# A convolution and attention network on one core: the steps of all engines in another order

## The reference

```python
# block 1 (after a group norm of 32 channels a group), n = 1024 pixels
xn  = layernorm(x[:, :48])                       # over 48 channels, per pixel
q, k, v = split(bn(w_qkv @ xn))                  # 16, 16, 48 channels
attn = softmax(q.T @ k / 4)                      # 1024 x 1024 per image
y   = bn(w_proj @ relu(concat(v @ attn.T, x[:, 48:])))
# block 2 (after a second group norm)
q, k, v = qkv_w @ x                              # 8 heads of 24 channels, attention over channels
at  = softmax(l2norm(q) @ l2norm(k).T * temperature) @ v
conv_x  = depthwise3x3(conv1x1(v))
t       = conv1x1(at)                            # 32 channels
channel_map = conv1x1(t * conv1x1(mean(t)) * conv1x1(dw7x7_dilated3(dw3x3(t))))
x1, x2  = split(depthwise3x3(conv1x1(conv_x)))   # spatial branch, gelu(x1) * x2
out = proj(at gated by the spatial map + conv_x gated by the channel map)
```

## Time and profile before

| | before |
|---|---|
| time, median of 3 runs | 395.75 us (395.29 to 396.08) |
| the profiled execution: span from first to last instruction | 393.8 us |
| its own time beside the span | not recorded; median less span is 1.95 us |
| TensorE busy | 353.9 us, 90% |
| VectorE busy | 269.3 us, 68% |
| ScalarE busy | 168.3 us, 43% |
| GpSimd busy | 24.1 us, 6% |
| DMA | 12.37 MB, mean 31 GB/s |
| chain that ended last | TensorE 75%, ScalarE 7%, VectorE 6%, SP's queue 4%, DMA 4% |

### The profile page before, as it was taken

One profiled execution on the slowest core, in us unless ns is written; L12 is line 12 of the kernel. 1 busy time (PEld: TensorE's weight loads), 2 busy tenths in 40 slices (PEclk: granted clock), 3 DMA queues, 4 the chain that ended last, 5 costly groups with the idle time before them and its releaser, 6 DMA issues.

```text
span 393.8 us, 5228 instructions
## 1 busy us (share of the span) xinstructions
PE 353.9 (90%) x2098; PEld 180.1 (46%) x2098; DVE 269.3 (68%) x490; ACT 168.3 (43%) x283; POOL 24.1 (6%) x29
## 2 busy tenths in 40 slices
PE   2978989999987998899999989998999889797995
PEld 1736644433465454544445465443244365352431
DVE  5757667551597647796878577889357889748553
ACT  2233054656503248346520775235522574625410
POOL 2030100000003200000000020000100001000000
PEclk9977689999997599999899999997999899969999
DMA  8450000000000001200002102000002111013005
GB/s 254 140 147 2 0 0 2 0 1 2 0 1 2 0 2 28 62 2 2 0 2 75 28 9 52 12 2 0 0 2 80 29 33 33 0 29 64 2 0 160
DMA packets 6069, 12.37 MB, mean 31 GB/s; under 512 B 2078, under 2 KB 2718, under 8 KB 5918
## 3 DMA queue, kind: packets, MB, share of 16 engines
q1 hardware_dynamic: 5532, 11.97, 11.2%
q10 hardware_dynamic: 514, 0.08, 0.1%
HBM read 5.32 MB, written 3.15 MB: 22 GB/s over the span
## 4 chain that ended last, share of the span: by engine, by line
PE 75%; ACT 7%; DVE 6%; SPq 4%; DMA 4%; POOL 2%; issue 1%; ACTq 0%
PE psO L616 5%; PE psR L791 5%; PE psA L606 4%; PE psA L587 3%; DVE nm L1374 2%; ACT pT L1980 2%; PE psB L659 2%; DMA x<-x_dram 2%; PE psB L680 2%; PE psS L616 2%; SPq L391 2%; DMA up<-up 2%; PE psA L564 2%; PE psA L791 2%; PE psO L544 2%
## 5 line engine op out<-in xcount | busy, mean ns | idle before, releaser
L1510 DVE SCALAR_TENSOR_TENSOR cx<-cpA,dw2w,cx 128x1024 f32<-128x1024 f32 x32 | 40.9, 1278 | 2.4 <-ACT cx L2012 2.4
L1521 DVE SCALAR_TENSOR_TENSOR dd<-spp,wt,dd 112x1024 f32<-112x1024 f32 x32 | 41.0, 1282 | 1.0 <-ACT dd L2093 0.3
L1980 ACT ACTIVATE pT<-psA 128x1024 f32<-128x1024 f32 x24 | 24.6, 1023 | 26.2 <-PE psA L606 26.0
L1374 DVE TENSOR_REDUCE nm<-psA 128x1 f32<-128x1024 f32 x20 | 24.5, 1223 | 12.2 <-PE psA L587 11.9
L616 PE MATMUL psO<-pT,vt 128*64 128x512 f32 x96 | 28.7, 678 | 0.1
L1510 DVE SCALAR_TENSOR_TENSOR cx<-cpB,dw2w,cx 128x512 f32<-128x512 f32 x32 | 23.8, 743 | 0.5 <-ACT cx L2012 0.5
L791 PE MATMUL psR<-up,wb 128*32 128x256 f32 (+1 forms) x336 | 20.9, 383 | 1.4 <-DMA up<-up 1.3
L606 PE MATMUL psA<-qs,ks 98*128 98x512 f32 x48 | 19.4, 488 | 2.1 <-ACT pT L1980 1.4
L587 PE MATMUL psA<-ks,qs 96*128 96x512 f32 x40 | 15.0, 456 | 3.2 <-DVE nm L1374 1.9
L606 PEld LDWEIGHTS psA<-qs,ks 98*128 98x128 f32 x48 | 8.1, 209 | 19.8 <-ACT pT L1980 16.2
L1310 DVE BATCH_NORM_STATS2 st<-x 128x6 f32<-128x512 f32 x24 | 15.7, 684 | 1.8 <-DMA x<-x_dram 1.6
(11 more groups left out here) (423 smaller groups left out, 735.9 us busy)
## 6 DMA issues: line engine op xcount, KB each, us to landing
up<-up SPq DMA_DIRECT2D x12, 200.0 KB, 3.1
x<-x_dram SPq DMA_DIRECT2D x4, 512.0 KB, 6.5
out_dram<-x SPq DMA_DIRECT2D x8, 256.0 KB, 2.1
wt<-params_dram SPq DMA_DIRECT2D x1, 1151.5 KB, 8.5
tp<-tp SPq DMA_DIRECT2D x8, 136.0 KB, 2.4
...
wt<-params_dram SPq DMA_DIRECT2D x1, 213.5 KB, 2.6
```

The lines of the kernel that those rows point to most:

```text
L1374: v.tensor_reduce(s.nm[:, t:t + 1], score_ps[b][t % 2][:], AX_X, ALU.max, negate=True).then_inc(nm_s.of(b), 1)
L1510: v.scalar_tensor_tensor(acc, img, dw2w[:, blk, tap:tap + 1], acc, ALU.mult, ALU.add).then_inc(cv_s.of(c), 1)
L1521: v.scalar_tensor_tensor(acc, t.spp[:, dy:dy + HH, dx:dx + WW], par("w_spdw")[:, tap:tap + 1], acc, ALU.mult, ALU.add).then_inc(dv_s.of(c), 1)
L1980: a(s.pT[t % 2][:], s.scoreT_ps[:], ACT.Exp).then_inc(ex_s.of(b), 1)
```

## The change

All changed lines are lines of the five call lists; no step is changed, added or left out, and every step waits for and signals what it did before. Some 225 of the calls stand in another place. The core of the diff:

```diff
@@ SP @@
   load_biases()
   shift_t(0)
   shift_u(0)
+  shift_t(1)
   store(0)
-  shift_t(1)
   shift_u(1)
+  shift_t(2)
   store(1)
-  shift_t(2)
   shift_u(2)
   shift_t(3)
   shift_u(3)
...
@@ TensorE @@
+  group_means(0, 0)
   keep_warm()
   keep_warm()
-  group_means(0, 0)
+  setup_ln()
   keep_warm()
   keep_warm()
   keep_warm()
   keep_warm()
   center(0)
   setup_qkv()
-  keep_warm()
   pixel_var(0)
   keep_warm()
-  setup_bias()
   keep_warm()
   rstd_rows(0)
-  group_means(0, 1)
+  keep_warm()
+  setup_bias()
   qk_product(0, 0)
   qk_product(0, 1)
   v_product(0)
+  group_means(0, 1)
   keep_warm()
   keep_warm()
   score_rows(0, 0)
   score_rows(0, 1)
-  center(1)
   score_rows(0, 2)
-  pixel_var(1)
+  setup2()
   score_rows(0, 3)
   score_rows(0, 4)
+  center(1)
   score_rows(0, 5)
+  pixel_var(1)
   score_rows(0, 6)
   score_rows(0, 7)
-  setup2()
   rstd_rows(1)
   max_rows(0)
   setup2_proj()
+  scores_t(0, 0)
   qk_product(1, 0)
   qk_product(1, 1)
-  scores_t(0, 0)
+  scores_t(0, 1)
+  pv(0, 0)
   v_product(1)
+  scores_t(0, 2)
   score_rows(1, 0)
   score_rows(1, 1)
-  scores_t(0, 1)
-  pv(0, 0)
+  pv(0, 1)
+  scores_t(0, 3)
   score_rows(1, 2)
-  scores_t(0, 2)
...
   denominator_rows(1)
   transpose_x(0, 0)
   transpose_x(0, 1)
+  transpose_x(0, 2)
   proj1(1)
-  transpose_x(0, 2)
   gram_x(0)
   group_means(1, 1)
   group_means(0, 2)
   gram_w(0)
   center(2)
+  head_scores(0)
   pixel_var(2)
-  head_scores(0)
   norms(0)
   rstd_rows(2)
   k_norm_rows(0)
   qk_product(2, 0)
   sp_in(0)
+  qk_product(2, 1)
   transpose_attn(0)
+  v_product(2)
   attn_weights(0)
   t_weights(0)
-  qk_product(2, 1)
-  v_product(2)
+  score_rows(2, 0)
   conv1_a(1)
-  score_rows(2, 0)
   t_product(0)
   score_rows(2, 1)
   conv1_b(1)
   score_rows(2, 2)
+  ci1_product(0)
   transpose_x(1, 0)
+  transpose_x(1, 1)
   score_rows(2, 3)
-  transpose_x(1, 1)
-  ci1_product(0)
+  ci2a(0)
+  score_rows(2, 4)
...
+  scores_t(2, 3)
   pv(2, 1)
-  scores_t(2, 3)
   pv(2, 2)
-  head_scores(1)
   scores_t(2, 4)
   pv(2, 3)
+  scores_t(2, 5)
+  head_scores(1)
+  norms(1)
   ci2b(0, 6)
-  scores_t(2, 5)
   pv(2, 4)
-  norms(1)
-  sp_out_a(0)
   scores_t(2, 6)
   map_mean(0)
   pv(2, 5)
   scores_t(2, 7)
+  k_norm_rows(1)
...
   group_means(0, 3)
+  sp_in(1)
   t_weights(1)
-  sp_in(1)
   center(3)
-  t_product(1)
   conv1_a(2)
   pixel_var(3)
   conv1_b(2)
+  transpose_x(2, 0)
+  t_product(1)
   rstd_rows(3)
-  transpose_x(2, 0)
   transpose_x(2, 1)
-  ci1_product(1)
   transpose_x(2, 2)
   qk_product(3, 0)
...
   conv1_b(3)
   transpose_x(3, 0)
   transpose_x(3, 1)
+  ci2a(2)
   transpose_x(3, 2)
-  ci2a(2)
   gram_x(3)
...
-  head_scores(3)
   ci2b(2, 0)
   ci2b(2, 1)
+  head_scores(3)
   norms(3)
   ci2b(2, 2)
   ci2b(2, 3)
-  sp_out_a(2)
   ci2b(2, 4)
   ci2b(2, 5)
+  k_norm_rows(3)
   ci2b(2, 6)
-  k_norm_rows(3)
   sp_in(3)
   transpose_attn(3)
+  map_mean(2)
   attn_weights(3)
   t_weights(3)
-  map_mean(2)
+  sp_out_a(2)
   t_product(3)
   attended_a(2)
   ci1_product(3)
...
   ci2b(3, 2)
   ci2b(3, 3)
   ci2b(3, 4)
-  sp_out_a(3)
   ci2b(3, 5)
   ci2b(3, 6)
+  sp_out_a(3)
   map_mean(3)
...
@@ VectorE @@
+  setup_slot1()
+  setup_ln()
   setup_zeros()
-  setup_ln()
   group_matrices()
   channel_stats(0, 0, 0)
   channel_stats(0, 0, 1)
   channel_stats(0, 0, 2)
   moments(0, 0)
+  setup2_a()
+  group_stats(0, 0)
+  group_shift(0, 0)
   channel_stats(0, 1, 0)
-  group_stats(0, 0)
   channel_stats(0, 1, 1)
-  group_shift(0, 0)
   channel_stats(0, 1, 2)
   setup_qkv()
-  setup_slot1()
+  pixel_var(0)
+  moments(0, 1)
   setup_weights()
-  pixel_var(0)
+  setup2_b()
+  layer_norm(0)
   setup_bias()
-  setup2_a()
-  moments(0, 1)
-  channel_stats(0, 2, 0)
-  layer_norm(0)
-  group_stats(0, 1)
-  setup2_b()
-  group_shift(0, 1)
   q_low(0)
   k_low(0)
   v_copy(0)
   row_max(0, 0)
+  group_stats(0, 1)
   row_max(0, 1)
+  group_shift(0, 1)
   row_max(0, 2)
   row_max(0, 3)
   row_max(0, 4)
+  row_max(0, 5)
   pixel_var(1)
-  row_max(0, 5)
   row_max(0, 6)
   row_max(0, 7)
   split_max(0)
   setup2_c()
   layer_norm(1)
...
-  channel_stats(0, 2, 1)
   channel_stats(0, 2, 2)
   moments(0, 2)
-  channel_stats(0, 3, 0)
-  channel_stats(0, 3, 1)
-  channel_stats(0, 3, 2)
-  setup2_e()
   inverse_denominators(0)
   attn_relu(0)
+  setup2_e()
   block1_out(0, 0)
-  moments(0, 3)
+  block1_out(0, 1)
+  channel_stats(0, 3, 0)
   channel_stats(1, 0, 0)
   channel_stats(1, 0, 1)
...
-  conv2(0, 4)
   channel_stats(1, 1, 2)
   moments(1, 1)
-  conv2(0, 5)
   conv2(0, 6)
+  conv2(0, 7)
   group_stats(1, 1)
   gram_copy(0, 0)
   gram_copy(0, 1)
-  group_shift(1, 1)
   group_stats(0, 2)
-  conv2(0, 7)
+  conv2(0, 8)
...
+  group_shift(1, 1)
   scaled_scores(0)
+  q_low(2)
   softmax_divide(0)
-  q_low(2)
+  normed(1)
+  k_low(2)
   copy_wma(0)
   copy_wmc(0)
-  normed(1)
-  k_low(2)
   v_copy(2)
   row_max(2, 0)
+  sp_conv(0, 0)
+  sp_conv(0, 1)
   pad_t(0)
   row_max(2, 1)
   row_max(2, 2)
+  ci1_scale(0)
   row_max(2, 3)
...
-  gram_copy(1, 0)
-  gram_copy(1, 1)
-  row_max(2, 7)
-  split_max(2)
-  sp_conv(0, 0)
-  sp_conv(0, 1)
-  sp_conv(0, 2)
-  ci1_weights(0)
   sp_conv(0, 3)
   sp_conv(0, 4)
+  conv2(1, 3)
+  times_w(1)
   sp_conv(0, 5)
   conv2(1, 4)
+  sp_conv(0, 6)
   conv2(1, 5)
-  sp_conv(0, 6)
   sp_conv(0, 7)
-  times_w(1)
-  gelu_product(0, 0)
-  gelu_product(0, 1)
-  channel_product(0)
-  clamp_norms(1)
-  inverse_norms(1)
   conv2(1, 6)
   conv2(1, 7)
   conv2(1, 8)
+  ci1_weights(0)
+  channel_product(0)
+  gelu_product(0, 0)
+  gelu_product(0, 1)
+  clamp_norms(1)
+  moments(0, 3)
...
   conv2(2, 10)
   conv2(2, 11)
   conv2(2, 12)
+  gate_attended(1, 0)
+  gate_attended(1, 1)
+  gate_attended(1, 2)
+  merge(1, 0)
+  merge(1, 1)
   clamp_norms(2)
+  inverse_norms(2)
+  merge(1, 2)
+  scaled_scores(2)
+  softmax_divide(2)
   conv2(2, 13)
-  inverse_norms(2)
-  scaled_scores(2)
...
+  conv2(3, 8)
   times_w(3)
-  conv2(3, 8)
-  gelu_product(2, 0)
-  gelu_product(2, 1)
-  clamp_norms(3)
   conv2(3, 9)
   conv2(3, 10)
   conv2(3, 11)
+  clamp_norms(3)
+  conv2(3, 12)
   inverse_norms(3)
-  conv2(3, 12)
   conv2(3, 13)
   conv2(3, 14)
   conv2(3, 15)
   scaled_scores(3)
+  ci1_weights(2)
   softmax_divide(3)
-  ci1_weights(2)
   channel_product(2)
+  gelu_product(2, 0)
...
@@ ScalarE @@
   load_small()
+  zero_back(0, 0)
+  zero_back(0, 1)
+  zero_back(0, 2)
+  zero_front(0)
+  zero_front(1)
+  zero_back(0, 3)
+  zero_front(2)
   setup_ln()
-  zero_front(0)
-  zero_back(0, 0)
-  zero_front(1)
-  zero_back(0, 1)
+  zero_back(0, 4)
+  zero_back(0, 5)
+  zero_front(3)
   normed1(0)
   squares(0)
-  rstd_copy(0)
   relu_normed(0, 0)
   relu_normed(0, 1)
+  zero_front(4)
+  zero_back(0, 6)
+  zero_front(5)
+  zero_front(6)
+  rstd_copy(0)
   q_high(0)
+  zero_front(7)
   k_high(0)
-  zero_front(2)
   normed1(1)
+  relu_normed(1, 0)
   squares(1)
   rstd_copy(1)
-  zero_front(3)
   max_copy(0)
+  exps(0, 0)
   q_high(1)
...
-  conv2_first(1, 1)
+  relu_normed(2, 0)
   copy_xT(1, 0)
   copy_xT(1, 1)
+  pad_ci2a(0)
   copy_xT(1, 2)
-  relu_normed(2, 0)
-  pad_ci2a(0)
-  sp_first(0)
+  conv2_first(1, 0)
+  conv2_first(1, 1)
+  max_copy(2)
...
   copy_tu(1, 0)
+  exps(2, 0)
   copy_tu(1, 1)
-  max_copy(2)
-  exps(2, 0)
   exps(2, 1)
   exps(2, 2)
   exps(2, 3)
   exps(2, 4)
+  exps(2, 5)
   gelu(0, 0)
   gelu(0, 1)
-  exps(2, 5)
   exps(2, 6)
+  exps(2, 7)
+  spatial_tanh(0, 0)
+  spatial_tanh(0, 1)
+  attn_out(2)
   channel_gate(0)
-  spatial_tanh(0, 0)
-  exps(2, 7)
-  attn_out(2)
-  spatial_tanh(0, 1)
   copy_k_norms(1)
...
-  q_high(3)
+  gelu(1, 0)
   k_high(3)
+  gelu(1, 1)
   pad_ci2a(1)
   copy_tu(2, 0)
+  relu_normed(3, 1)
   copy_tu(2, 1)
-  relu_normed(3, 0)
-  gelu(1, 0)
-  gelu(1, 1)
   spatial_tanh(1, 0)
   spatial_tanh(1, 1)
   channel_gate(1)
   spatial_tanh(1, 2)
-  max_copy(3)
   attended_bias(1, 0)
   attended_bias(1, 1)
-  attended_bias(1, 2)
+  max_copy(3)
   exps(3, 0)
   exps(3, 1)
+  attended_bias(1, 2)
...
-  gelu(2, 0)
+  copy_k_norms(3)
   gelu(2, 1)
+  head_exps(3)
+  copy_attT(3)
+  channel_gate(2)
+  copy_wmt(3)
+  pad_sp(3, 0)
   spatial_tanh(2, 0)
   spatial_tanh(2, 1)
-  copy_k_norms(3)
-  head_exps(3)
-  pad_sp(3, 0)
+  pad_t(3)
   pad_sp(3, 1)
-  copy_attT(3)
   sp_first(3)
-  copy_wmt(3)
-  channel_gate(2)
-  pad_t(3)
   copy_t(3)
+  attended_bias(2, 0)
+  attended_bias(2, 1)
   pad_ci2a(3)
   spatial_tanh(2, 2)
+  attended_bias(2, 2)
   gelu(3, 0)
   gelu(3, 1)
-  attended_bias(2, 0)
-  attended_bias(2, 1)
-  attended_bias(2, 2)
...
```

More of the change, by code:

```diff
@@ L1114, in _ @@
             proj1(3)
-            transpose_attn(2)
             sp_in(2)
@@ L1590, in _ @@
             layer_norm(1)
+            channel_stats(0, 2, 0)
             setup2_d()
@@ L1594, in _ @@
             v_copy(1)
+            channel_stats(0, 2, 1)
             row_max(1, 0)
@@ L1798, in _ @@
             result(1, 2)
-            softmax_divide(2)
+            conv2(2, 14)
+            conv2(2, 15)
             block1_out(3, 0)
```

193 lines of the change are left out of this document (90 added, 103 removed).

## The result

The changed kernel takes **376.5 us** (median of 4 executions, 374.69 to 379.85) against 395.52 for the kernel before (4 executions): a ratio of 0.953, interval 0.9466 to 0.9596. The forecast was 387.8 with a range down to 381.5, so the sign was right and the size was not: 19 us came where 8 were forecast.

The account below looks back on a forecast made before the run. TensorE, busy 90% of the span at clock 0.930, was taken as the bound, except in the start and single gaps. Start +0.4, gaps -7.6, balance -0.8 sum to -8.0 us: time 387.8, range 381.5 to 396.5.

Parts of the forecast that it names:

- the later gaps: Eight TensorE waits from 121.37 us on, each worth at most its idle time: -7.6 us, and -0.8 for the balance.
- 270.50: scores_t(3, 1) waits 1.36 us for the first exp; attended_bias(1, 2) goes behind the second exp: -1.3 us.
- The clock pays too: Rival: closing gaps at 121.37 and 270.50 also spares 13.6 us at half clock; 382 us, chance 0.18.
- The start: Setup chain over all engines: later gav load and moved steps against savings, +0.4 us, bounds -3 and +5.
- 164.51: ci2b(0, 0) waits 1.35 us for shifted copies of up; ci2a(0) and pad_ci2a(0) move ahead: -1.3 us.
- 343.42: attn_weights(3) waits 1.26 us for the copied attention, behind pad_sp(3, 0) and (3, 1): -0.9 us.
- 229.75: rstd_rows(3) waits 0.88 us for GpSimd's power; a transpose and t_product(1) now stand ahead: -0.9 us.
- 317.15: The last transposes wait 0.96 us for the copy of cpB; ci2a(2) goes ahead of the last one: -0.9 us.
- 121.37: center(2) waits 1.66 us for ScalarE's xa; a transpose goes ahead and group_shift(1, 1) moves away: 0.7 us taken off.
- The start costs all that it can: Rival: gav lands near the 8.5 bound and setup2 runs at half clock, +5 us; 392.3 us, chance 0.12.
- the gaps move and do not close: Rival: the gaps move, or the compiled order differs less than the text; 395.5 us, chance 0.06.
- The clock takes more: Rival: steps between 35 and 120 or 137 and 188 us fall to half clock; 399.8 us, chance 0.14.

Follow-up runs that it names:

- early_undo: The run early with ScalarE's attended_bias(1, 2) put back ahead of exps(3, 0): 376.5 us.
- early: The changed kernel with VectorE's setup_zeros first again and ScalarE's setup_ln right behind its loads: 371.55 us.
- start_new: Every engine's order up to about 85 us from the changed kernel, the rest from the kernel before: 392.4 us.
- start_old: Every engine's order up to about 85 us from the kernel before, the rest from the changed kernel: 379.9 us.

## Why the prediction was wrong

**The failed step** is in the part on the later gaps: "each is worth no more than that", the idle time in front of one step. A gap is also worth what it does to the clock behind it. For the gap of 1.36 us at 270.50 the prediction had -1.3; brought back alone in early_undo it cost 5.0 against early. Closed alone in the kernel before it gave nothing that the interval shows, because the wait came back 16 us on. The sum held the clock at 0.93 and put the whole of it into a rival ("The clock pays too", 382 us, chance 0.18) that spared 13.6 us at half clock in two places. Measured were 41.9 us less, in all parts of the span: in the two profiles 17 in the first 60 us, which the rival left out, 10 in the middle and 14 in the last third. That term is 15 us where the forecast had 0 and the rival 5.5. The chances were out of proportion too: the rival in which the clock gets worse had 0.14, nearly as much, though the change's whole effect, fewer and shorter waits at the places in question, speaks for the other side.

The Trainium skill, TensorE: Matmul & The Clock Gate, part on the clock gate, says that activity releases the throttle and idleness brings it back. The runs agree: the clock fell behind the wait of 1.36 us in early_undo and not without it in early, and eleven small matmuls in the start were worth 8.4 us.

**The start** was forecast at +0.4 with bounds of -3 and +5. At equal clock it is +1.5 (start_new), or +2.9 if taken from after and start_old, so the bounds held. In its steps: center(0) at 21 was 21.37, the q product at 28 was 28.79. VectorE's first steps ended 0.5 us later than summed, and the gav load landed in 5.5 us, not 4.7, so the first copy came at 10.22 instead of 8.9. The same load took 3.6 to 4.9 us in the other runs, so a difference of 0.8 can be spread. And a wait of 3.10 us for bn2h was missed: setup2_a stands ahead of group_stats(0, 0) in the new order and held it until 18.00, though its product was done by 16.2. The bn2h load is the last that ScalarE issues behind the memset. The queue of loads was read for gav alone. The Trainium skill, DMA: Bandwidth & Descriptors, section on the anatomy of one DMA, gives the fixed part of about 2 us that the prediction quotes for transfers issued by GpSimd. This load is issued by ScalarE, and the figure had no part in the sum. scores_t(0, 0) came at 49.16, not near 53; most of its way there ran at the full clock, setup2 in 1.9 us where it took 3.5. The two calls put back in early were worth 5 us, 4.2 at equal clock.

**The gaps** were forecast at -7.6 - 0.8; at equal clock the middle and the last third give 1.9 + 2.7 = 4.6 one by one, and 7.7 together (start_old). Closed as forecast: 123.17, 164.51, 270.50, 343.42; 229.75 went to 0.42. Not closed: 317.15 (0.96 again, at 301.55), 338.88 (0.65), and 121.37 grew to 2.09. There ScalarE's xa starts at 115.60 and runs 1.65 us; it waits for VectorE's group_shift at 115.40, and that for GpSimd's power of 1.67 us (1.14 before). From the last group mean to center(2) it takes 4.3 us now and 3.9 before, with the same two products between, so the moves of the change did not shorten this chain. New ones took their place: 1.10 at 122.62 and 0.57 at 180.99. The idle time behind the first 30 us fell by 4.4. TensorE's whole idle time was forecast to fall to 33 us; it is 40.9, since the start took 5.4 more.

**The other rivals.** "The start costs all that it can" did not come; "the gaps move and do not close" was half true (idle time unchanged) and told nothing about the time, because its price left out the clock as well. "The clock takes more" found no support.

The forecast had said what would prove it wrong: a span that shrinks by over 11 us, or a clock that leaves 0.91 to 0.94. Both happened.
